# Values, own-token products and projection of two batches taken together, once per pair

## What is computed

```python
# L2: q, k, v, norm, rotary and the update of the cache come first
scores = jnp.einsum('bghtd,bgsd->bghts', qg, k_all) * SCALE
scores = jnp.where(allowed[:, None, None, :, :], scores, -jnp.inf)
p = jax.nn.softmax(scores, axis=-1)
o = jnp.einsum('bghts,bgsd->bghtd', p, v_all).reshape(Bx, H, Tx, HD)
...
return jnp.einsum('bto,do->btd', o, Wo)          # added to x
# L3
out = jnp.einsum('bct,bcd->bdt', x, weights[subjects])
out = out + bias[subjects][:, :, None]           # added to x
```

## Time and profile before

| | |
|---|---|
| median of 3 runs | 934.08 us (932.72 to 934.34) |
| profiled execution, its own time | 935.61 us |
| its span | 933.8 us |
| PE matmul busy | 890.7 us (95%) |
| PE weight load busy | 654.8 us (70%) |
| DVE busy | 648.5 us (69%) |
| ACT busy | 442.8 us (47%) |
| POOL busy | 529.0 us (57%) |
| TensorE clock granted, mean | 0.991 |

### The profile page before, as it was taken

How to read it: one execution, slowest core, us unless ns; L and a number is a source line. 1 busy time by engine, 2 the same in 40 slices (tenths; PEclk the granted TensorE clock), 3 DMA queues, 4 the chain that set the end, 5 groups by cost and what they waited for, 6 DMA issues and landing times.

```text
span 933.8 us, 23545 instructions
## 1 busy us (share of the span) xinstructions
PE 890.7 (95%) x6501; PEld 654.8 (70%) x6501; DVE 648.5 (69%) x1858; ACT 442.8 (47%) x1190; POOL 529.0 (57%) x499
## 2 busy tenths in 40 slices
PE   5599999999999999999996899999999999999997
PEld 3357667666666676676676677878778778777785
DVE  3545445778787764466755778888778887787874
ACT  1424333333333333333423666666666676666762
POOL 2044655655746557865467666655666656666630
PEclk9889999999999999999999999999999999999999
DMA  9999988787887978887716766676766776666741
GB/s 285 300 285 333 332 303 294 258 286 258 264 291 241 295 252 273 307 269 263 250 64 214 209 205 193 194 211 189 214 194 193 210 222 206 198 199 202 227 133 47
DMA packets 100417, 218.55 MB, mean 234 GB/s; under 512 B 30187, under 2 KB 36168, under 8 KB 92178
## 3 DMA queue, kind: packets, MB, share of 16 engines
q1 hardware_dynamic: 66290, 145.27, 47.4%
q0 software_dynamic: 25088, 57.74, 21.5%
q10 hardware_dynamic: 8992, 15.00, 4.4%
HBM read 210.39 MB, written 33.86 MB: 262 GB/s over the span
## 4 chain that ended last, share of the span: by engine, by line
PE 77%; DVE 7%; DMA 6%; SPq 3%; issue 3%; ACTq 2%; ACT 2%; POOL 1%; DVEq 0%; POOLq 0%
PE banks L697 14%; PE banks L847 9%; PE banks L610 9%; PE banks L799 9%; PE banks L835 7%; PE banks L822 6%; PE banks L678 5%; PE banks L776 4%; DMA pair_b<-in_lb 4%; PE banks L883 3%; PE banks L840 3%; DVE later L1166 2%; PE banks L663 2%; PE banks L777 1%; PE banks L815 1%
## 5 line engine op out<-in xcount | busy, mean ns | idle before, releaser
L569 POOL DMA_INDIRECT ring<-new_rows,idx x128 | 129.3, 1010 | 81.1 <-PE banks L799 45.8
L1050 ACT ACTIVATE big<-big,neg_max 128x320 f32<-128x320 f32 x256 | 141.5, 555 | 4.7 <-DVE neg_max L1417 4.4
L1417 DVE CUSTOM_DVE_ANT_0 big<-banks,mask 128x320 f32<-128x320 f32 x256 | 114.6, 486 | 23.6 <-PE banks L799 22.5
L610 PE MATMUL banks<-ring 128*64 128x512 f32 x512 | 119.5, 609 | 11.5 <-DMA ring<-in_w 11.5
L497 POOL TENSOR_TENSOR rms<-ss,neg_half 128x12 f32<-128x12 f32 x30 | 68.5, 2283 | 70.3 <-DVE ss L1356 70.3
L1040 ACT ACTIVATE kt<-banks 128x384 f32<-128x384 f32 x128 | 61.8, 483 | 92.9 <-PE banks L777 92.8
L495 POOL TENSOR_TENSOR ring<-ring 128x512 f32<-128x512 f32 x30 | 38.7, 1291 | 87.4 <-DVE ring L1237 87.4
L558 POOL DMA_INDIRECT ring<-new_rows,idx x64 | 61.5, 961 | 47.0 <-PE banks L822 42.7
L799 PE MATMUL banks<-kt,q_in 64*128 64x128 f32 (+2 forms) x768 | 86.7, 358 | 1.3 <-ACT kt L1040 1.3
L1454 DVE TENSOR_SCALAR big<-big,recip 128x320 f32<-128x320 f32 x256 | 85.7, 397 | 2.3
L610 PEld LDWEIGHTS banks<-ring 128*64 128x64 f32 x512 | 35.0, 140 | 68.8 <-issue 67.5
(11 more groups left out here) (172 smaller groups left out, 2011.3 us busy)
## 6 DMA issues: line engine op xcount, KB each, us to landing
ring<-in_w SPq DMA_DIRECT2D x62, 1024.0 KB, 8.0
ring<-in_xt SPq DMA_DIRECT2D x32, 256.0 KB, 2.7
x_in<-in_x SPq DMA_DIRECT2D x32, 256.0 KB, 5.8
bias_in<-in_b SPq DMA_DIRECT2D x64, 128.0 KB, 8.0
x_dram<-x SPq DMA_DIRECT2D x32, 256.0 KB, 8.8
q_dram<-q_t ACTq DMA_DIRECT2D x32, 256.0 KB, 6.5
new_rows<-kv_out SPq DMA_DIRECT2D x32, 256.0 KB, 6.4
q_in<-q_dram SPq DMA_DIRECT2D x32, 256.0 KB, 2.8
```

The costliest lines, as they stand in the source:

```text
L569: pool.indirect_dma_start(out=kv[:, s, c, :], out_offset=None, in_=new_rows, in_offset=bass.IndirectOffsetOnAxis(ap=idx[:, b, 1 + c:2 + c] ...
L610: last = nc.tensor.matmul(ps_l0[T * h:T * h + T, :], xt[:, s, c, T * h:T * h + T], w0[:, 2 * s + h, c * D:(c + 1) * D], start=(c == 0), st ...
L1050: nc.scalar.activation(prob[:, s % 2, PLACE[g] * NK:(PLACE[g] + 1) * NK], sm[:, s % 2, g, :], ACT.Exp, bias=neg_max[:, s % 2, g:g + 1], sc ...
L1417: V.tensor_tensor_reduce(sm[:, s % 2, g, :], ps_s[g], mask[:, s % 2, k0:k0 + NK], 1.0, 3.0e38, ALU.add, ALU.min, accum_out=neg_max[:, s % ...
```

## The change

Values and own-token products no longer run once per batch but once per pair, in the even iteration, behind `mix`; the values' output holds both batches side by side (two runs of 64 columns each, in one group of 128 rows x 256 columns per bank). The probabilities' copies pt and pt2 get a second slot, one per batch of the pair. ot_hi and ot_lo are made once per pair with 512 columns, at the start of the odd iteration. All 12 matmuls of the projection stand in the odd iteration. On VectorE x3 moves to the start of the even iteration and x4 from the odd to the even one; the place of `copy_first` among the masks changes too. On ScalarE `early` is now four in odd iterations and one in even ones. The transposes of the very last batch's probabilities go to two other banks.

```diff
-        pt = sb("pt", [P, 2, 2, 2, P])
-        pt2 = sb("pt2", [P, 2, P])
+        pt = sb("pt", [P, 2, 2, 2, 2, P])
+        pt2 = sb("pt2", [P, 2, 2, P])
...
-        ps_o = [ps[4 + p][:, 0:P] for p in range(GP)]
+        ps_o = [ps[4 + p][:, 0:2 * P].rearrange("p (c h t) -> p c h t", c=2, h=2) for p in range(GP)]
...
+        def pairs(b, j, s, slots):
+
+            return b // 2 if isinstance(b, int) else j * (slots // 2) + s // 2
+
+        def prob_banks(b):
+
+            return ps[0:2] if isinstance(b, int) and b == NB - 1 else ps_pt
...
-                    pool.wait_ge(pv_done, PV_INCS * (b - KV_SLOTS + 1))
+                    pool.wait_ge(pv_done, (b - KV_SLOTS) // 2 + 1)
...
-                    wait(pe, ot_ready, b - 1)
+                    wait(pe, ot_ready, m if odd else m - 1)
...
-                                nc.tensor.matmul(ps_o[p][HD * q:HD * q + HD, :], kv[:, r, c, v0:v0 + HD], pt[:, p, PLACE[2 * p + q] % 2, c, :],
-                                                 start=(c == 0), stop=False, skip_group_check=True)
...
+                                nc.tensor.matmul(ps_o[p][HD * q:HD * q + HD, :, h, :], kv[:, v, c, v0:v0 + HD],
+                                                 pt[:, h, p, PLACE[2 * p + q] % 2, c, :],
+                                                 start=(c == 0 and h == 0), stop=False, skip_group_check=True)
...
-                behind_probs = isinstance(b, int) and b == NB
-                if second_half and not behind_probs and not is_last(pair):
-                    project(range(DC // 2, DC), ps_x).then_inc(wo_done, 1)
...
-                        project(range(DC // 2), ps_x)
...
+                        project(range(DC), ps_x).then_inc(wo_done, 1)
+                if not odd and on(b, 4, NB):
+                    mix()
+                if not odd and on(b, 2, NB):
+                    values(0)
+                    values(1)
+                    own_values()
...
+                if odd and on(b, 3, NB):
+
+                    act.wait_ge(pv_done, m)
+                    wait(act, wo_done, m - 2)
+                    nc.scalar.activation(ot_hi[:, (s // 2 + 1) % 2, :, :].rearrange("p (g c) t -> p g (c t)", g=GP), o_view,
+                                         ACT.Copy).then_inc(othi_ready, 1)
...
-                early = 1 if s % 2 == 1 or ramp else G
+                early = G if odd and not ramp else 1
...
+                if not odd and on(b, 4, NB):
+                    add_x3()
+                if odd and on(b, 3, NB):
+                    split_outputs()
                 if on(b, 0, NB):
+                    dve.wait_ge(mask_ready, b + 1)
+                    masked(0)
                     masked(1)
-                if s % 2 == 1 and on(b, 1, NB):
+                    if not odd:
+                        masked(2)
+                if on(b, 1, NB):
                     copy_first()
                 if on(b, 0, NB):
-                    masked(2)
+                    if odd:
+                        masked(2)
                     masked(3)
...
+                if not odd and on(b, 4, NB):
+                    add_x4()
```

More of the change, by code:

```diff
@@ L785, in phase_two @@
                 r = (s - 1) % KV_SLOTS
-                first_half, second_half = s % 2 == 1 and on(b, 3, NB), s % 2 == 0 and on(b, 4, NB)
-                pair = (b // 2 if isinstance(b, int) else j * (KV_SLOTS // 2) + s // 2) - (1 if s % 2 else 2)
+                m = pairs(b, j, s, KV_SLOTS)
+                odd = s % 2 == 1
+                pair = m - 1 if odd else m - 2
                 pair_s = (s // 2 + s % 2) % 2
@@ L849, in project, with mix @@
                     return last
+                def mix():
+                    pe.wait_ge(ld_pair[pair_s], PAIR_DMAS * 16 * (j * 2 + s // 4))
+                    for i, (n0, n1) in enumerate(COLUMN_PARTS if is_last(pair) else WHOLE):
+                        pe.wait_ge(x3_ready, pair + 1 + i)
+                        nc.tensor.matmul((ps_mix[i] if is_last(pair) else ps_x)[:, n0:n1], bd[:, pair_s, :], x3[:, pair_s, n0:n1],
+                                         start=True, stop=True).then_inc(l3_done, 1)
                 if on(b, 0, NB):
@@ L1080, in phase_two @@
                     copy_keys(b + 1, s + 1, 1)
[L1081 to L1090, removed]
+            loop(act, phase_two, 4, 4, NB + 2, NB - 4)
         @block.vector
@@ L1394, in phase_two @@
             def phase_two(b, j, s):
+                m = pairs(b, j, s, 4)
+                odd = s % 2 == 1
+                pair, pair_s = m - 2, s // 2
                 def copy_first():
                     dve.wait_ge(pt_done, 3 * b - 1)
-                    wait(dve, pv_done, b - 1)
-                    V.tensor_copy(pt[:, 0, :, :, :].rearrange("p q c t -> p (q c t)"), ps_pt[0][:, :]).then_inc(pt0_ready, 1)
+                    wait(dve, pv_done, m if odd else m - 1)
+                    V.tensor_copy(pt[:, (s - 1) % 2, 0, :, :, :].rearrange("p q c t -> p (q c t)"), prob_banks(b - 1)[0][:, :]).then_inc(
+                        pt0_ready, 1)
@@ L1401, in split_outputs @@
                 def split_outputs():
-                    dve.wait_ge(othi_ready, b)
-                    h, t = (s - 1) % 2, ((s - 1) % 4) // 2
-                    o_lo, o_hi = (o[:, t, :, T * h:T * h + T].rearrange("p (g c) t -> p g c t", g=GP) for o in (ot_lo, ot_hi))
+                    dve.wait_ge(pv_done, m)
+                    dve.wait_ge(othi_ready, m)
+                    o_lo, o_hi = (o[:, (s // 2 + 1) % 2, :, :].rearrange("p (g c) t -> p g (c t)", g=GP) for o in (ot_lo, ot_hi))
                     V.tensor_tensor(o_lo, o_view, o_hi.bitcast(F32), ALU.subtract).then_inc(ot_ready, 1)
-                added, finished = s % 2 == 0 and on(b, 4, NB), s % 2 == 1 and on(b, 5, NB)
@@ new lines, in add_x4 @@
+                def add_x4():
+                    wait(dve, st_out[pair_s], 16 * (j - 1))
+                    for i, (n0, n1) in enumerate(COLUMN_PARTS if is_last(pair) else WHOLE):
+                        dve.wait_ge(l3_done, pair + 1 + i)
+                        dve.wait_ge(x3_ready, pair + 1 + i)
+                        V.scalar_tensor_tensor(x4[:, pair_s, n0:n1], (ps_mix[i] if is_last(pair) else ps_x)[:, n0:n1], sbias[:, pair_s, 0:1],
+                                               x3[:, pair_s, n0:n1], ALU.add, ALU.add).then_inc(x4_ready, 1)
@@ L1456, in phase_two @@
                     make_mask(b + 1, s + 1)
[L1457 to L1460 removed]
+            loop(dve, phase_two, 4, 8, NB + 3, NB - 4)
 def kernel(x, itok_B_0_15, itok_B_0_6, itok_Bx257_0_4111, itok_B_37_3939, itok_B_0_7, fside_8xS_0, L0_cond_W, L0_cond_b,
```

80 lines of the change are left out of this document (31 added, 49 removed).

## The result

The changed kernel took 927.66 us in the median of seven executions (922.53 to 929.10), the kernel before 933.91 in seven beside it (931.42 to 936.61): ratio 0.9913, 95% interval 0.9888 to 0.9938. Run once more in a later group it gave 0.9883 (0.9839 to 0.9926). So it is faster, by about 1%. The ratios are formed over the runs of a group and not from the two medians; they stand for 8 and 11 us, the differences of the medians for 6.3 and 10.3. The forecast was 932.0 us, 2.1 us faster, and named rival 1 with 927.1.

The account below looks back on a forecast made before the run. PE's instruction stream was taken to bound the second half. 29 pairs at 12.83 for 12.86 us gave -0.9, the tail -1.2, the ramp 0: 2.1 us off 934.08, so 932.0 us, range 926.6 to 936.5.

Parts of the forecast that it names:

- rival 1: Odd iteration: PE waits for nothing, the key copy coming 0.17 us earlier; pair 12.66, total 927.1 us; chance 0.15.
- new wait of the odd iteration: End of odd iteration: PE waits 0.17 us for ScalarE's key copy before the next scores, 6.17 instead of 6.00 us.
- What bounds the kernel: Second half: PE's instruction stream sets the time, a pair costing 12.86 us; the even iteration's ScalarE copy within 0.1 us.
- The projection's move: Six projection matmuls go from the even to the odd iteration on PE: 1.41 us saved and added, net zero.
- Values and own products: Even iteration on PE: two batches together take 2.60 us for 2.80, saving 0.20 us per pair.
- theory A: Hypothesis of the follow-up runs: in odd iterations PE waits for the key copy ending the chain the prediction laid out.
- Tail: After the last scores: 0.65 us earlier from x4 leaving the masks and 0.54 us less afterwards, together -1.2 us.
- Ramp: First iterations: values and projection shift to iterations 2 and 3; taken as 0, with 1.4 us to either side.
- Rival 2: Odd iteration: the probabilities' copy between masks 1 and 2 waits 0.32 us instead of 0.1; 938.4 us; chance 0.14.
- Rival 3: Even iteration: the 0.20 us gaps are not tile changes, so it stays at 6.86; about 937.8 us; chance 0.05.
- Rival 4: Values and own products: split output runs double their time, 2.6 us more per pair, 1014 us; chance 0.02.

Follow-up runs that it names:

- the two runs with the shorter chain: Changed kernel with one early exponential in odd iterations too, 922.81 us; changed kernel with mask 2 ahead of the probabilities' copy in odd iterations, 922.78 us.
- the second profile: The changed kernel unaltered, run and profiled once more in a later group: 924.52 us.
- the alternating order: Changed kernel with the pair's groups ordered values, own products, values, own products instead of values twice, own products twice: 933.50 us, ratio 0.9995.

## Why the prediction was wrong, point by point

Two terms of its sum had the wrong size, the saving of pairing on PE and the new wait of the odd iteration; the path was the one that it laid out.

- **What bounds the kernel** was right: PE's stream, and the even iteration level with the ScalarE copy (0.02 to 0.03 us of waiting).
- **The projection's move is neutral on PE**: right. Without waits odd is 5.99 as forecast (6.00), and the unknown step from projection to scores is 0.33 (the two runs with the shorter chain), the value kept.
- **Values and own products**: the term failed in size. I took 0.14 between the halves of the own products and 0.18 for the second half. In the trace the own products start in fours; only between the first four and the second four behind a change of tiles are there 0.14, later 0.09, so the halves are 0.09 apart and the second one takes 0.13. All 16 records take 0.60 and not 0.70 (729.22 to 729.82), and the step from the mix to the values is 0.95 and not 0.98. Saving 0.30 instead of 0.20, and the copy's wait of 0.02 to 0.03 besides, which the forecast had counted as PE's own: even 6.54 for 6.66.
- **The new wait in the odd iteration**: the mechanism was right, to the copy between the masks, and lengthening and shortening it moved the odd iteration as theory A said. Its size was wrong. Every step between instructions came out within 0.01; what I had too long were the two signals, PE to VectorE 0.1 for 0.04 and ScalarE to PE 0.12 for 0.05. The second I had read as "at most" and then used as if it were the value; in the earlier trace rows the key copy ended 0.12 before the scores and PE's own stream set their start, so that row bounded the signal and did not measure it. The first came from x3 in the tail, another instruction behind another kind of matmul. The wait is 0.05 and not 0.17.
- Together: pair 12.58 for 12.83, 0.25 us on each, 7 us on 28 pairs. This is the whole miss.
- **Tail**: right, -1.20 for -1.2. In the changed kernel x4 is gone from the masks and the last pair's split is exposed:

```profile
912.56 0.44 PE L823 MATMUL banks<-ident,big 128*128 128x128 f32 x2 [0.77 <-DVE big L1481]
...
917.29 0.60 ACT L1087 ACTIVATE ot_hi<-banks 128x512 fp32r<-128x512 f32 x1 [2.79 <-PE banks L856]
...
917.99 0.69 DVE L1428 TENSOR_TENSOR ot_lo<-banks,ot_hi 128x512 fp32r<-128x512 f32 x1 [2.42 <-ACT ot_hi L1087]
...
918.74 0.38 PE L863 MATMUL banks<-wo_hi,ot_hi 128*128 128x256 f32 x1 [1.51 <-DVE ot_lo L1428]
```

  912.56 to 918.74 is 6.18 us (forecast 6.17; 6.71 in the earlier trace rows).
- **Ramp**: right at +0.05 where the clock held (36.66 us to batch 6 in the second profile, 36.61 before), in part by luck: iteration 1 is 0.98 shorter (6.07 for 7.05) and not 1.40, iteration 2 is 1.53 longer, and the next ones give the rest back.
- **Rivals**: rival 1's time, 927.1, was the better forecast, and its mechanism nearly right: PE waits for almost nothing. That its time met the median so closely is partly luck: its pair of 12.66 is still 0.07 too long, and the change was worth 10.3 us and not 7.0 in the later group. Its chance of 0.15 rested on the difference of 0.17 in the chain, of which the term from ScalarE to PE, a bound from above, could only err on one side. Rival 2 decides from a signal of 0.17 on and measured 0.04. Rival 3 fell with the alternating order. Rival 4 fell with the rows: 32 value records into split runs take 1.97, (1.97 - 0.27) / 31 = 0.055 each, as in the contiguous form. The rule of the Trainium skill ("PSUM — Partial Sum Buffer", section Specifications) that the prediction weighed did not hold here for runs of 64 columns.

## What to carry to other kernels

Group matmuls of the same tile shape: on a stream bound by PE each change of shape cost 0.15 us, and two changes fewer per pair were worth 28 x (12.907 - 12.593) = 8.8 us here, 0.9%. When work moves on the bound engine, move what feeds it as well: x3 and the order of the exponentials, left in place, each cost some 40 us (x3 about 1.3 us per pair, the order 1.5). And where a forecast turns on 0.1 us in a chain, ask of each term whether its row measures it or only bounds it; a consumer that was not waiting gives a bound.

## What was not expected of the hardware

Signals between engines were shorter here than I took: 0.04 us from the end of a transpose (by the profile's modelled end) to VectorE's copy, 0.05 to 0.06 from ScalarE's copy to PE's weight load. The masks' 0.32 behind the scores is not the signal alone: in iteration 7, where the waits have fixed numbers and no register instruction stands between them, the first mask starts 1.52 behind the scores' start (555.22 behind 553.70) and not 1.68, so at least 0.16 of it is the register instruction and the wait behind it. A VectorE copy of 80 columns shows 0.30 us and holds up the next instruction by 0.11. And the granted clock in the ramp differs between executions of one kernel: 0.57 and 1.00 over the same 4 us, worth 1.5 us in the first iteration, after 2.95 and 1.25 us of idle time for the same gather.
